# First attention of a two-layer kernel: input rows loaded turned, centring moved from the rows into the query weights

## The reference, cut to what matters

```
q     = rmsnorm(LN(x) @ Wq.T + bq) * qn_w          # per row of 512
c_n   = rmsnorm(ctx) * fn_w
k     = rmsnorm(c_n @ Wk.T + bk) * kn_w
x     = x + softmax(q @ k.T / sqrt(512), within blocks of 64 rows) @ c_n
```

## Time and profile before

| | |
|---|---|
| median of three runs | 1511.28 us |
| lowest, highest | 1510.58, 1512.31 us |
| the profiled run | 1511.27 us, span 1509.5 us |
| PE, DVE, ACT, POOL busy | 97%, 75%, 53%, 47% of the span |
| first attention | 0 to about 178 us of the span |

### The profile page before, as it was taken

One profiled execution on the slowest core, in us unless ns is written; L12 is line 12 of the kernel. 1 busy time (PEld: TensorE's weight loads), 2 busy tenths in 40 slices (PEclk: granted clock), 3 DMA queues, 4 the chain that ended last, 5 costly groups with the idle time before them and its releaser, 6 DMA issues.

```text
span 1509.5 us, 27579 instructions
## 1 busy us (share of the span) xinstructions
PE 1463.2 (97%) x9895; PEld 846.4 (56%) x9895; DVE 1127.8 (75%) x2172; ACT 795.1 (53%) x3201; POOL 710.3 (47%) x668
## 2 busy tenths in 40 slices
PE   5999999999999799999999999999999999999998
PEld 4888745555555455555555555555565555555554
DVE  5788787878876888776776676677677677667868
ACT  5678841211223576556546654754664565565763
POOL 5668875454565353334334343433434333343553
PEclk9999999999999999999999999999999999999999
DMA  7454435333344565653553554455445445334622
GB/s 248 147 175 136 123 81 126 98 77 50 65 88 72 117 147 84 110 119 64 100 105 53 95 88 81 86 87 95 81 80 105 79 73 103 64 60 67 99 50 112
DMA packets 358936, 146.87 MB, mean 97 GB/s; under 512 B 342304, under 2 KB 342688, under 8 KB 356112
## 3 DMA queue, kind: packets, MB, share of 16 engines
q1 hardware_dynamic: 357504, 137.77, 45.1%
q10 hardware_dynamic: 1296, 7.34, 1.5%
HBM read 58.02 MB, written 4.19 MB: 41 GB/s over the span
## 4 chain that ended last, share of the span: by engine, by line
PE 55%; DVE 5%; ACT 3%; DMA 1%; POOL 1%; issue 1%; SPq 0%; DVEq 0%; POOLq 0%; ACTq 0%
PE bank L72 18%; PE bank L74 17%; PE bank L73 17%; PE bank L2439 3%; ACT a_prob L1836 2%; DMA a_pT_lo<-a_p_lo 1%; POOL a_prob L1707 1%; DVE a_oT_lo L2106 1%; DVE x_res L2193 1%; DVE a_qve L2045 1%; ACT a_oT_lo L1813 0%; DVE a_p_lo L2094 0%; DVE a_nmx L2082 0%; DVE a_qr_lo L2035 0%; POOL a_xr_lo L1731 0%
## 5 line engine op out<-in xcount | busy, mean ns | idle before, releaser
L1836 ACT ACTIVATE a_prob<-a_prob,a_nmx 128x64 f32<-128x64 f32 x512 | 170.2, 334 | 183.7 <-DVE a_nmx L2082 183.7
L72 PE MATMUL bank<-w,a_oT_hi 128*128 128x512 f16 x512 | 194.0, 379 | 1.8 <-DVE a_oT_lo L2106 0.9
L74 PE MATMUL bank<-w,a_oT_hi 128*128 128x512 f16 x512 | 194.0, 379 | 0.0
L73 PE MATMUL bank<-w,a_oT_lo 128*128 128x512 f16 x512 | 194.0, 379 | 0.0
L72 PE MATMUL bank<-w,xT_hi 128*128 128x448 f16 (+1 forms) x512 | 188.0, 367 | 3.1 <-DVE h L1231 2.0
L73 PE MATMUL bank<-w,xT_lo 128*128 128x448 f16 (+1 forms) x512 | 187.7, 367 | 0.0
L74 PE MATMUL bank<-w,xT_hi 128*128 128x448 f16 (+1 forms) x512 | 187.5, 366 | 0.0
L1707 POOL TENSOR_TENSOR a_prob<-a_prob,a_mask 128x512 f32<-128x512 f32 x64 | 79.8, 1268 | 204.5 <-DVE a_prob L2076 204.5
L2031 DVE SCALAR_TENSOR_TENSOR x_res<-bank,a_oinv,x_res 128x512 f32<-128x512 f32 x128 | 95.5, 746 | 75.0 <-PE bank L74 75.0
L1157 ACT CAST f_h_hi<-h 128x448 f16<-128x448 f32 x64 | 35.6, 563 | 209.7 <-DVE h L1231 209.6
L1719 POOL TENSOR_TENSOR a_krs<-a_kve,neg_half 128x4 f32<-128x4 f32 x32 | 32.8, 1026 | 239.6 <-DVE a_kve L2056 239.6
(11 more groups left out here) (351 smaller groups left out, 4120.5 us busy)
## 6 DMA issues: line engine op xcount, KB each, us to landing
shared<-in_l_wq SPq DMA_DIRECT2D x8, 1024.0 KB, 5.0
shared<-in_l_wo SPq DMA_DIRECT2D x8, 1024.0 KB, 5.1
shared<-in_w ACTq DMA_DIRECT2D x8, 896.0 KB, 4.7
craw<-in_w SPq DMA_DIRECT2D x11, 512.0 KB, 3.9
a_wide<-in_l_ctxT SPq DMA_DIRECT2D x16, 256.0 KB, 4.0
x_res<-in_x SPq DMA_DIRECT2D x16, 256.0 KB, 4.5
shared<-in_ctx SPq DMA_DIRECT2D x16, 256.0 KB, 4.4
shared<-in_l_wkv SPq DMA_DIRECT2D x8, 512.0 KB, 3.9
```

Source lines behind the costliest of these rows:

```text
L72: pe.matmul(out, a_hi, b_hi, start=first, stop=False)
L73: pe.matmul(out, a_lo, b_hi, start=False, stop=False)
L74: return pe.matmul(out, a_hi, b_lo, start=False, stop=last)
L1836: ins = act.activation(pt, pt, ACT.Exp, bias=nmx[:, col:col + 1], accum_out=den[:, col:col + 1])
```

## The change

The layer norm of the rows is taken apart. Since (x - mean) @ W.T = x @ (W - column mean of W).T, the mean is taken out of the query weights once, on the chip; since the row scale rs is a factor of the whole row, it is applied after the projection. So the raw rows can be projected, and they are loaded from memory a second time, already turned (`l0_xT`, laid out by the host as `l0_ctxT` is), 256 KB per tile into two buffers `xT_raw`.

- Gone: normalise on ACT, the four transposes per tile on PE, the shift on POOL, the bank `bxT`.
- Changed: ACT's rows_T reads `xT_raw` instead of the bank; DVE's rows_T subtracts the high part from `xT_raw`, so both its inputs lie in SBUF; query_bias is (bank * rs) + bias and waits for rs; `sums` is doubled, and each wait for it is one tile looser; SP sends `xT` of each tile behind its x.
- New at the start: POOL adds pairs of blocks of wq (`add_wq`), DVE adds the two sums, PE multiplies by a 128 x 128 tile of 1/512 (`thin`), which gives the column mean in every partition, and DVE subtracts it from the four blocks (`centre_wq`) before they are split. project_k(1) goes ahead of project_q(0), project_q(1) and key_bias(1) move ahead of the loop, and several loads change places.

```diff
+        def load_xT(n):
+            if n:
+                sp.wait_ge(xT_in, n * 16)
+            sp.dma_start(xT_raw[n % 2][:, :, :], a.l0_xT[n]).then_inc(xT_in, 16)
...
+            sp.wait_ge(s_xTl, n - 1)
+            load_xT(n)
...
-            if n >= 2:
-                pool.wait_ge(s_xn, min(n + 2, NT))
-            pool.tensor_scalar(sh2[:, (n + 3) % 2:(n + 3) % 2 + 1], sums[:, 0:1], -1.0, three[:, 0:1], ALU.mult, ALU.mult)\
-                .then_inc(s_root, 1)
+            pool.tensor_tensor(three, three, m.neg_half[:, 0:3], ALU.pow).then_inc(s_root, 1)
+
+        def add_wq(out, half):
+            pool.wait_ge(wq_in[half], 16)
+            pool.tensor_tensor(out, w_raw[0][:, 2 * half, :], w_raw[0][:, 2 * half + 1, :], ALU.add).then_inc(s_mean, 1)
...
-            act.activation(xn[:, :], m.x[:, bass.ts(n, D)], ACT.Identity, bias=sh(n), scale=rs(n)).then_inc(s_xn, 1)
...
-            act.copy(xT_hi[:, :, :], blk(bxT)).then_inc(s_xTh, 1)
+            act.wait_ge(xT_in, (n + 1) * 16)
+            if n:
+                act.wait_ge(s_q, n)
+            act.copy(xT_hi[:, :, :], xT_raw[n % 2][:, :, :]).then_inc(s_xTh, 1)
...
-            dve.tensor_tensor(xT_lo[:, :, :], blk(bxT), xT_hi[:, :, :], ALU.subtract).then_inc(s_xTl, 1)
+            dve.tensor_tensor(xT_lo[:, :, :], xT_raw[n % 2][:, :, :], xT_hi[:, :, :], ALU.subtract).then_inc(s_xTl, 1)
...
-            dve.tensor_tensor(qb[:, :], bq_bank[:, :], bq, ALU.add).then_inc(s_qb, 1)
+            wait_rows_root(dve, n)
+            if n:
+                dve.wait_ge(s_qss, n)
+            dve.scalar_tensor_tensor(qb[:, :], bq_bank[:, :], rs(n), bq, ALU.mult, ALU.add).then_inc(s_qb, 1)
...
+        def centre_wq(k):
+            dve.tensor_tensor(w_raw[0][:, k, :], w_raw[0][:, k, :], w_mean[:, :], ALU.subtract).then_inc(s_mean, 1)
...
-        rows_T(0)
-        project_q(0, first=True)
+        pe.wait_ge(s_mean, 3)
+        pe.matmul(w_mean[:, :], thin[:, :], w_sum, start=True, stop=True).then_inc(s_mean, 1)
         pe.wait_ge(s_kb, 1)
         project_k(1)
-        q_T(0)
+        project_q(0, first=True)
         k_T(0)
-        rows_T(1)
+        q_T(0)
+        project_q(1)
```

More of the change, by code:

```diff
@@ L193, in sem @@
         return a0_sems[-1]
-    bq_bank, bk_bank, bxT, b_prep, bqT, bkT, b_s, b_att = m.bank
+    bq_bank, bk_bank, _, b_prep, bqT, bkT, b_s, b_att = m.bank
     b_pT = b_s[:, P:2 * P]
@@ L205, in l0_attention @@
     off = sb("off", [P, P])
-    wide = sb("wide", [P, 7 * D])
-    xn, cw, kn, qb, kb = (wide[:, n * D:(n + 1) * D] for n in range(5))
+    wide = sb("wide", [P, 8 * D])
+    cw, kn, qb, kb = (wide[:, n * D:(n + 1) * D] for n in range(1, 5))
+    xT_raw = [wide[:, n * D:(n + 1) * D].rearrange("p (k f) -> p k f", k=KD) for n in (0, 7)]
     cT_raw = [wide[:, n * D:(n + 1) * D].rearrange("p (k f) -> p k f", k=KD) for n in (5, 6)]
@@ L390, in tile_roots @@
             three = root4[:, n % RING, :]
-            pool.tensor_tensor(three, sums[:, 1:4], eps3[:, :], ALU.add).then_inc(s_rve, 1)
+            pool.tensor_tensor(three, sums[:, n % 2, 1:4], eps3[:, :], ALU.add).then_inc(s_rve, 1)
             pool.wait_ge(s_rve, next(roots))
-            pool.tensor_tensor(three, three, m.neg_half[:, 0:3], ALU.pow).then_inc(s_rve, 1)
-            pool.wait_ge(s_rve, next(roots))
-            if n >= 2:
-                pool.wait_ge(s_xn, min(n + 2, NT))
-            pool.tensor_scalar(sh2[:, (n + 3) % 2:(n + 3) % 2 + 1], sums[:, 0:1], -1.0, three[:, 0:1], ALU.mult, ALU.mult)\
-                .then_inc(s_root, 1)
+            pool.tensor_tensor(three, three, m.neg_half[:, 0:3], ALU.pow).then_inc(s_root, 1)
+        def add_wq(out, half):
+            pool.wait_ge(wq_in[half], 16)
+            pool.tensor_tensor(out, w_raw[0][:, 2 * half, :], w_raw[0][:, 2 * half + 1, :], ALU.add).then_inc(s_mean, 1)
         def features_lo(n):
@@ L446, in pool_steps @@
         features_T(0)
-        first_row_root(0)
+        add_wq(w_sum, 0)
+        add_wq(w_high, 1)
         first_features_root(0)
@@ L559, in body @@
                 squares_c(n + 2)
-                normalise(n + 2)
                 features_T(n + 2)
@@ L602, in act_steps @@
             act.activation(w_hi[1][:, k, :], w_raw[1][:, k, :], ACT.Copy, scale=fnw_T[:, k:k + 1]).then_inc(wh_ok, 1)
[L604 to L610 removed]
         squares_c(0)
         rows_T(0)
[L613 removed]
         features_T(1)
[L615 to L616 removed]
         key_squares(0)
+        for k in range(KD):
+            act.wait_ge(s_mean, 5 + k)
+            act.copy(w_hi[0][:, k, :], w_raw[0][:, k, :]).then_inc(wh_ok, 1)
+        act.dma_start(w1_raw[0], a.w1[:, 0:W1P]).then_inc(w1_in[0], 16)
         squares_c(1)
[L619 removed]
+        rows_T(1)
         qk_T(0)
         query_squares(0)
[L622 removed]
         features(0)
+        act.dma_start(w1_raw[1], a.w1[:, W1P:2 * W1P]).then_inc(w1_in[1], 16)
         run(body)(act)
@@ L666, in body @@
         def body(n, first=False, ahead=True, project=True):
-            if project:
+            if project and not first:
                 key_bias(n + 1)
@@ L774, in split_wk, with split_wq @@
                                          ALU.mult, ALU.subtract).then_inc(wl_ok, 1)
-        def split_wq(ks):
-            for k in ks:
-                dve.wait_ge(wh_ok, KD + k + 1)
-                dve.tensor_tensor(w_lo[0][:, k, :], w_raw[0][:, k, :], w_hi[0][:, k, :], ALU.subtract).then_inc(wl_ok, 1)
+        def centre_wq(k):
+            dve.tensor_tensor(w_raw[0][:, k, :], w_raw[0][:, k, :], w_mean[:, :], ALU.subtract).then_inc(s_mean, 1)
+        def split_wq(k):
+            dve.wait_ge(wh_ok, KD + k + 1)
+            dve.tensor_tensor(w_lo[0][:, k, :], w_raw[0][:, k, :], w_hi[0][:, k, :], ALU.subtract).then_inc(wl_ok, 1)
         split_wk((0, 1))
-        statistics(0)
         split_wk((2, 3))
-        split_wq((0, 1))
-        rows_T(0)
-        split_wq((2, 3))
+        dve.wait_ge(s_mean, 2)
+        dve.tensor_tensor(w_sum, w_sum, w_high, ALU.add).then_inc(s_mean, 1)
         dve.wait_ge(bk_in, 16)
         key_bias(0)
+        rows_T(0)
+        dve.wait_ge(s_mean, 4)
+        centre_wq(0)
+        centre_wq(1)
+        split_wq(0)
+        centre_wq(2)
+        split_wq(1)
+        centre_wq(3)
+        split_wq(2)
+        split_wq(3)
         dve.wait_ge(const_in, 48)
-        statistics(1)
         dve.scalar_tensor_tensor(wqk, qnw[:, :], float(D) ** -0.5, wqk, ALU.mult, ALU.mult).then_inc(wqk_ok, 1)
+        statistics(0)
         dve.wait_ge(wqk_ok, 1)
@@ L795, in dve_steps @@
         query_bias(0)
+        rows_T(1)
+        statistics(1)
+        key_bias(1)
         qk_T(0)
-        rows_T(1)
         statistics(2)
@@ L804, in pe_steps @@
     def pe_steps(pe, filler):
-        def rows_T(n):
-            pe.wait_ge(s_xn, n + 1)
-            for k in range(KD):
-                ins = pe.transpose(bxT[:, k * P:(k + 1) * P], xn[:, k * P:(k + 1) * P], m.ident[:, :])
-            ins.then_inc(s_xT, 1)
         def project_k(n, first=False):
@@ L862, in body @@
             ins.then_inc(s_s, 1)
-            if first:
-                project_q(n + 1)
-            if ahead:
-                rows_T(n + 2)
             if not first:
@@ L2628 @@
         "l0_ctxT": ctx_rows.reshape(NT, P, KD, P).transpose(0, 3, 2, 1),
+        "l0_xT": given["x"].reshape(NT, P, KD, P).transpose(0, 3, 2, 1),
         "l0_fnwT": given["L0_xattn_fn_w"].reshape(KD, P).T,
```

76 lines of the change are left out of this document (32 added, 44 removed).

## The result

The changed kernel took 1523.03 us (median of four runs, 1520.77 to 1524.33), the kernel before 1510.93 in the runs beside it: a ratio of 1.0081, 95% interval 1.0066 to 1.0095. It is slower by 12 us, where 6.2 had been forecast, and above the upper end of the range, 1521.5.

The account below looks back on a forecast made before the run. Two paths from the scores to k_T, PE's work and VectorE's mask to scale_keys, were taken to tie at 1.60 us. Terms 0 + 4.9 + 1.3 = +6.2 on 1511.27 gave 1517.5 us; range 1510.4 to 1521.5.

Parts of the forecast that it names:

- The row transposes leave PE: Loop: removing four transposes per tile (0.38 us) gains 0, since k_T still waits for scale_keys; ends 0 and -4.9.
- Activation and GpSimd lose a step: Loop: without normalise and shift, the chain is shorter in a few tiles where GpSimd holds scale_keys: -1.2 us.
- The row split is held: Loop, VectorE: split with two SBUF inputs waits for GpSimd's running features_lo, ending at 58.53 instead of 57.68: +0.85 us.
- By tiles: Loop: VectorE's +0.92 us per tile against its slack, priced tile by tile: +4.9 net, the -1.2 included.
- four more tiles at 0.2: Late loop tiles: VectorE has slack, but late GpSimd is held some 0.45 us against 0.27 saved: +0.8 together.
- The start: Ahead of the loop: centring of wq delays the third feature tile and k_T(1); +1.3 us, ends -1 and +4.7.
- SP sends the third feature tile ...; hence 33.2: Start: feature load sent at 29.6 instead of 25.77, its data used 3.6 us later as before, at 33.2.
- about half of the 2.5: Start: of k_T(1)'s 2.5 us delay, about half returns because work moved behind the low-clock stretch runs at twice the speed.
- Behind the loop: After the last loop mask: no term; the extra 256 KB per tile were to cost nothing later: 0.
- rival 3: PE granted 1.2 GHz over one more stretch of 6.8 us: 3.4 us more than forecast, 1521; chance 0.12.

Follow-up runs that it names:

- bank_transposes: after_bank with four transposes per tile put back on TensorE behind the scores of the first 14 tiles, output overwritten: 1513.83 us.
- after_bank: Changed kernel, but from tile 2 on the row split subtracts from a zero-filled PSUM bank instead of the raw rows in SBUF: 1514.44 us.
- best2: Changed kernel with the early weight pieces of after_loads, and Activation's rows_T ahead of its exponential: 1513.16 us.
- after_nocentre: Changed kernel without the centring of wq (the mean stays in the rows): 1522.59 us.
- after_loads: Changed kernel, but Activation sends both 896 KB weight pieces ahead of the splits of wq: 1519.37 us.
- before_late_piece: Kernel before with the second 896 KB weight piece sent later; meant ahead of the third feature tile, it went out behind it: 1511.35 us.
- best4: best2, and in turns 1 to 3 the row split on GpSimd and the keys scaled ahead of the mask, as in best1: 1510.93 us.
- best1: after_loads; turns 1 to 5: row split on GpSimd, keys scaled ahead of the mask; other turns: features_lo waits as in after_order: 1514.50 us.
- after_order: Changed kernel, but in the loop GpSimd's features_lo waits until VectorE's row split of the same turn is done: 1517.15 us.

## Why the prediction was wrong

The direction, the main mechanism and its place were right; the size was half, and the range ended 1.5 us too low. Step by step:

- **The row transposes leave PE: 0.** Right, to 0.03 us (bank_transposes). The 97% for PE would have said 4.9.
- **Activation and GpSimd lose a step: -1.2.** Right in size: 1.11 us of gain are left in the loop when the split is not held (after_bank). The division over the tiles was partly luck: two tiles that follow each other are 0.54 shorter and 0.20 longer than before.
- **The row split is held: right in mechanism and price** (1.50 us, ending 0.55 behind features_lo). The Trainium skill's rule (SBUF — State Buffer, "Who interferes with whom") is what the runs show, its order of issue included: the second to come waited in both directions (60.98 in the kernel after, 57.23 in best2). By the whole duration behind the release the split would have ended 0.14 us later than it did; there the measurement decides. The same section makes an exception from its single-input rule for copies and TENSOR_SCALAR in two-port modes, which the prediction left out; a copy and a TENSOR_SCALAR were held here (last section), and in which mode they ran no run shows.
- **By tiles: +4.9, measured +6.06.** The first three tiles cost 0.60, 0.57 and 0.60 (forecast 0.64 each), the fourth 0.93 (0.9). The fifth cost 0.83 instead of 0.3, and the ninth, forecast at +0.9 as bound by VectorE, is 0.54 shorter than before; its split is not held (129.56, 0.69 us). The first nine come to 3.23 where 4.1 was forecast. (The list prices twelve of the fourteen intervals: the sixth and one of the last five have no term.) The term that failed most is the last, four more tiles at 0.2 (+0.8), on the ground that VectorE has slack there: the last five intervals cost 2.83. The last three of them cost 0.61, 1.16 and 0.87. In after_bank the same three are 0.08, 0.07 and 0.06 shorter than before, so the excess comes with the held split: splits of 1.65, 1.50 and 1.74 us (148.50, 158.06, 168.44). With the splits, a small copy from SBUF to SBUF on VectorE came beside GpSimd's features_T and took 1.34 us instead of 0.23; I had looked for collisions of the split only, not of the VectorE operations that it displaces. The kernel after, then the kernel before:

```profile
163.80 1.28 POOL L422 TENSOR_TENSOR a_big<-a_wide,a_big 128x512 fp32r<-128x512 f32 x1
163.82 1.34 DVE L755 COPY wmax_b<-a_w_top 128x128 f32<-128x128 f32 x1
```

```profile
156.18 0.23 DVE L749 COPY wmax_b<-a_w_top 128x128 f32<-128x128 f32 x1
```

- **The start: +1.3, measured +3.37.** The step that failed is "SP sends the third feature tile ...; hence 33.2". It was sent at 29.04 (forecast 29.6), but used at 35.14: the 3.6 us of before were carried over as if nothing else were in the queues. Activation's two weight pieces, sent together from 15.20 on in the trace before, now stand apart, and go out at 20.01 and 28.62. I priced the moved instructions of VectorE and GpSimd and the new loads of SP, and overlooked the DMAs that moved on Activation. The centring, on which most of that part was spent, costs nothing that can be measured (after_nocentre). From the data to k_T(1) 5.2 us were forecast and 5.07 measured (35.14 to 40.21), and of the 4.29 us at k_T(1) 3.37 were left at the first mask: 0.92 returned, where about half of the 2.5 was to be. By the medians the place of the weight pieces is worth 3.7 us (after_loads).
- **Behind the loop: 0, measured +2.87.** A further stretch at 1.2 GHz was my rival 3, with 0.12, as something that happens in place of the forecast; it came beside it, and not behind the first tile but at the hand-over. Among the profiled runs, those with a granted clock of 1.00 in 162 to 198 have a rest of 1336.81 to 1338.15, those with 0.91 one of 1338.87 to 1342.63. It comes behind stretches in which PE idles (165 to 169, 177 to 181), and these are longer where VectorE is late. But it also came in best2 and in before_late_piece, whose loop is exactly that of before. In these two, in before and in best4 PE is busy for the same 1.63 or 1.64 of the 3.00 us ahead of the last mask; in the 3.00 us behind it the first two are granted 0.58 and 0.54, the other two 1.00. So the idle time there does not decide alone, and what makes the stretch come in one run and not in the next stays open.
- **The sum.** 3.37 + 6.06 + 2.87 = 12.30, 6.1 more than forecast: 2.1 at the start, 1.2 in the loop, 2.9 behind it. The first two have a cause that runs show (after_loads; after_bank), and in the medians these two edits, each run by itself, gave back 3.7 and 8.6 us. The 2.9 is the difference of two profiled runs; a stretch at 1.2 GHz goes with it, and what brings that stretch is open.

## What to carry to other kernels

When a change takes work off the busiest engine, ask which other path ends at the same instruction: here two paths tied at k_T to 0.07 us, and the work removed from one was worth nothing (bank_transposes); the early tiles fell below before's only where the other was shortened too (best1, best4). Moving an operand from PSUM to SBUF did not change the operation's own time (0.69 us in before and in after_order), but made it exclude another engine's; then who comes first decides who pays, and letting the one with the later reader wait is a mend that costs one reordered instruction (best2, a loop of 127.16 against 133.53). List every DMA that changes its place against the data which the start waits for, on all queues: here a transfer of 896 KB went out 0.4 us ahead of a small one that is waited for, and sending the two large pieces early gave back 3.7 us.
